# A retention and expert kernel on one core: shorter warm-up products, x by channels loaded from ScalarE's queue, two transfers at other points of SyncE's order

## What is computed

```python
x = x + attn(layernorm(x))     # q, k, v = x @ W.T; scores q.k times gamma_h ** (i - j) for j <= i, over sqrt(16)
                               # y = scores @ v; normalised over (time, channels of a head), scaled, shifted; @ W_o.T
x = x + ffn(layernorm(x))      # ((silu(x@sw1+sb1) * (x@sw3+sb3)) @ sw2 + sb2
                               #   + mean over k = 0, 1 of expert[(11*token + 7919*k) % 8](x)) / 2
# expert e: gelu(x @ w1[e] + b1[e]) @ w2[e] + b2[e]
```

## Time and profile before

| | before |
|---|---|
| median of three runs | 431.55 us (431.1 to 432.46) |
| the profiled execution | 431.59 us |
| its span, first to last instruction | 429.8 us |
| PE busy | 419.1 us, 98% of the span |
| DVE, ACT, POOL busy | 78%, 51%, 20% |
| granted TensorE clock | 9 tenths or more in all 40 slices |

### The profile page before, as it was taken

The page is one execution under the profiler, slowest core; times in us unless marked ns, Lnnn a source line. Parts: engine busy times, 40 slices in busy tenths (PEclk is TensorE's granted clock), DMA queues, the critical chain, the costliest instruction groups (busy, mean ns, idle before and its releaser), DMA issues.

```text
span 429.8 us, 14531 instructions
## 1 busy us (share of the span) xinstructions
PE 419.1 (98%) x6232; PEld 380.5 (89%) x6232; DVE 335.3 (78%) x791; ACT 219.2 (51%) x420; POOL 87.9 (20%) x78
## 2 busy tenths in 40 slices
PE   7998999999999989999999999999999999999997
PEld 5987899999998989998989988899888998888996
DVE  7888689876987788987798887978879878856423
ACT  3566667555754568345257325483344834346530
POOL 3062634532344232650510000100001000000000
PEclk9999999999999999999999999999999999999999
DMA  8554444434351232315450015100142001120011
GB/s 262 192 150 139 126 151 116 114 104 133 123 169 51 87 115 89 101 53 195 158 187 2 2 49 190 56 0 1 49 152 91 0 1 49 49 98 0 2 50 49
DMA packets 19769, 39.79 MB, mean 93 GB/s; under 512 B 3040, under 2 KB 5376, under 8 KB 19200
## 3 DMA queue, kind: packets, MB, share of 16 engines
q1 hardware_dynamic: 19280, 38.31, 27.5%
q10 hardware_dynamic: 432, 0.66, 0.5%
HBM read 30.55 MB, written 8.41 MB: 91 GB/s over the span
## 4 chain that ended last, share of the span: by engine, by line
PE 96%; issue 1%; DVE 1%; DMA 1%; POOL 0%; ACT 0%; DVEq 0%
PE bank L434 54%; PE bank L443 13%; PE bank L526 7%; PE bank L444 7%; PE bank L556 4%; PE bank L571 4%; PE bank L540 3%; PE bank L505 2%; PE bank L589 1%; DMA xin<-xa 1%; PE bank L647 0%; PE bank L461 0%; PE bank L452 0%; DVE xlo L1311 0%; DVE ln_st L1298 0%
## 5 line engine op out<-in xcount | busy, mean ns | idle before, releaser
L434 PE MATMUL bank<-x2lo,sw_hi 128*128 128x512 f32 x128 | 50.5, 394 | 0.0
L434 PE MATMUL bank<-x2hi,sw_lo 128*128 128x512 f32 x128 | 50.2, 392 | 0.0
L434 PE MATMUL bank<-x2hi,sw_hi 128*128 128x512 f32 x128 | 50.1, 392 | 0.0
L443 PE MATMUL bank<-w_both,ehi 128*128 128x512 f32 x124 | 45.1, 397 | 0.0
L887 ACT ACTIVATE sil<-bank,s1b 128x512 f32<-128x512 f32 x32 | 22.0, 687 | 45.0 <-PE bank L434 44.9
L443 PE MATMUL bank<-sw_both,ghi 128*128 128x512 f32 x124 | 44.9, 396 | 0.0
L1199 DVE STREAM_TRANSPOSE x2t<-xl 32x256 f32<-32x256 f32 x96 | 41.8, 436 | 1.8
L768 ACT ACTIVATE kexp<-bank 64x256 f32<-64x256 f32 x64 | 24.2, 378 | 30.9 <-PE bank L505 30.2
L1029 DVE TENSOR_TENSOR pm<-bank,msk 128x512 f32<-128x512 f32 x64 | 39.5, 679 | 0.0
L434 PE MATMUL bank<-xhi,wqkv_hi 128*128 128x256 f32 x128 | 38.0, 297 | 0.1
L906 ACT ACTIVATE ehi<-xres 128x512 fp32r<-128x512 f32 x32 | 20.3, 633 | 33.1 <-PE bank L444 32.6
(11 more groups left out here) (154 smaller groups left out, 1152.0 us busy)
## 6 DMA issues: line engine op xcount, KB each, us to landing
w_raw<-w SPq DMA_DIRECT2D x16, 256.0 KB, 3.3
xres<-xs SPq DMA_DIRECT2D x16, 256.0 KB, 3.4
x_scratch<-xres SPq DMA_DIRECT2D x16, 256.0 KB, 3.3
xl<-x_scratch SPq DMA_DIRECT2D x8, 512.0 KB, 4.5
xr<-x_scratch SPq DMA_DIRECT2D x4, 1024.0 KB, 4.8
xin<-xa SPq DMA_DIRECT2D x15, 256.0 KB, 3.0
out<-xr SPq DMA_DIRECT2D x7, 512.0 KB, 2.6
xin_t<-xt SPq DMA_DIRECT2D x13, 256.0 KB, 2.6
```

The costliest lines, as they stand in the source:

```text
L434: mm = nc.tensor.matmul(o, w[c][l], x[c][r], start=first and c == 0 and j == 0, stop=last and c == n - 1 and j == 2)
L443: nc.tensor.matmul(o.rearrange("p (k d) -> p k d", k=2), hi, w[c], start=c == 0, stop=c == n - 1, skip_group_check=True)
```

## The change

Four edits:

1. `WARM_UP` is 12 instead of 4, and each warm-up product has `CH` = 64 columns instead of 256.
2. `load_rstd(h + 2)` waits for `k_done` (k of part h + 1 projected) where it stood right behind the transfers of `sc_done`.
3. `load_xt` leaves SyncE, together with the wait for `kt_done`. ScalarE issues it in its step between `spread_k(h + 1)` and `copy_k(h + 1)`, with the same wait for `xlo_ready` from part 5 on.
4. In steps 8, 9, 12 and 13 the first of the two `next_xres` moves up from behind `y_done` to behind `q_done` and a new wait for `s_done` (the state sums of part h).

```diff
-WARM_UP = 4
+WARM_UP = 12
@@ block.sync
-            def load_xt(h):
-                if h >= TURNED + 2:
-                    sp.wait_ge(xlo_ready, h)
-                sp.dma_start(xin_t[h % 2][:], xt[h]).then_inc(xt_landed[h % 2], 16)
-
@@ block.sync, step(h)
                 if TURNED <= h + 2 < PARTS:
+                    sp.wait_ge(k_done, h + 2)
                     load_rstd(h + 2)
                 if h + 1 < PARTS:
                     sp.wait_ge(q_done, h + 2)
...
                     load_ffn(2 + LOAD_STEPS.index(h), 1)
-                if h + 1 < PARTS:
-                    sp.wait_ge(kt_done, h + 2)
-                if h + 3 < PARTS:
-                    load_xt(h + 3)
+                if b >= 2 and s < 2:
+                    sp.wait_ge(s_done, h + 1)
+                    next_xres(b - 1, 2 * s)
                 if h + 1 < PARTS:
                     sp.wait_ge(v_done, h + 2)
...
                 if b >= 2 and s < 2:
-                    next_xres(b - 1, 2 * s)
                     next_xres(b - 1, 2 * s + 1)
@@ block.tensor, warm_up(n)
-                    nc.tensor.matmul(c_bank[:, 0:2 * P], zeros[:, 0:P], zeros[:, 0:2 * P], start=True, stop=True)
+                    nc.tensor.matmul(c_bank[:, 0:CH], zeros[:, 0:P], zeros[:, 0:CH], start=True, stop=True)
@@ block.scalar
+            def load_xt(h):
+                if h >= TURNED + 2:
+                    act.wait_ge(xlo_ready, h)
+                act.dma_start(xin_t[h % 2][:], xt[h]).then_inc(xt_landed[h % 2], 16)
+
@@ block.scalar, step(h), behind spread_k(h + 1)
+                if h + 3 < PARTS:
+                    load_xt(h + 3)
                 if h + 1 < PARTS:
                     copy_k(h + 1)
```

## The result

The changed kernel takes 437.18 us (median of 6 runs, 434.63 to 439.19), the kernel before 431.16 in the same comparison. The ratio is 1.0143, 95% interval 1.0117 to 1.0170: **slower by 1.4%, 6 us**. I had forecast 430.8, so the sign was wrong and the time lies outside my range. The profiled execution has a span of 436.0 us (437.75 in all), against 429.8.

The account below looks back on a forecast made before the run. TensorE, busy 419.1 of 429.8 us, bounds the kernel, with 5.13 us lost to late instruction blocks. 431.59 - 0.9 (stops) + 0.15 (warm-up) = 430.8 us; own range 429.2 to 432.3, with rivals 427.6 to 433.6.

Parts of the forecast that it names:

- what the stops are: TensorE's "issue" gaps in the retention stage: late blocks of 256 instructions, 127 products apart; 5.13 us in all.
- The worst place I named: New short stretch of 2.15 us at 95.57, DMA share 0.62: a stop of 1.2 us near 97.7.
- My eight terms: Stops forecast for stretches at 19.73, 33.64, 36.60, 52.68, 70.59, 95.57, 127.97, 153.74; with 0.2 for two more, 4.2 us.
- x by channels on ScalarE: Issue of load_xt between spread_k and copy_k, in 13 steps: cost nothing, as ScalarE idles there for kt_done.
- the sum's main term: Late instruction blocks on TensorE, crossings 16 products earlier: stops 4.2 us against 5.13, so -0.9 us.
- warm-up as work: Start on TensorE: 24 records end near 6.3 where transposes began at 6.16, +0.15 us; bounds 0 and +1.1.
- rival B: Start: last warm-up product not far under 634 ns, transposes not started by 6.4; slower; chance 0.15.
- the shift: Warm-up count as instructions: every retention-stage crossing comes 16 products earlier, changing the stops by -0.9 us.
- My values lie between 0 and the bound: Each new stop valued between 0 and 5.2 us less its stretch, as a block needs 2.6 to 5.2 us.
- the moved transfers: load_rstd, next_xres and the waits: counted in the block needs, nothing of their own, between -0.5 and +0.5 us.

Follow-up runs that it names:

- e3: Changed kernel with the old warm-up (4 products of 256 columns) and 32 empty instructions behind it: 435.93 us, ratio 1.0132.
- e4: Kernel before with 32 empty instructions behind the warm-up, nothing else: 435.01 us, ratio 1.0106.
- e7: Kernel before with 16 empty instructions in front of TensorE's first wait, ahead of the warm-up: 434.36 us, ratio 1.0094.
- e8: Kernel before with load_xt moved to ScalarE's queue, without SyncE's wait for kt_done: 434.56 us, ratio 1.0091.
- the ladder: Ratios to before, adding edits: two moved transfers 0.9934; crossings 16 products earlier 1.0028; warm-up of 64 columns 1.0080; x early on ScalarE (changed kernel) 1.0143.
- the last pair of kernels: Changed kernel with load_xt held back on ScalarE by kt_done: warm-up of 64 columns 433.66 us (1.0080), of 128 columns 431.04 us (1.0028).
- e6: Kernel before with 12 warm-up products of 128 columns, no transfer moved: 433.42 us, ratio 1.0051.
- e10: Kernel before with load_xt on ScalarE's queue but behind the wait for kt_done, at its old time: 430.88 us, ratio 1.0003.
- e12: Kernel before with 4 warm-up products of 64 columns: 431.27 us, ratio 0.9992.

## Why the prediction was wrong, point by point

**Right: what the stops are.** The count of 127 products in a block, and that added instructions move the crossings 16 products earlier, hold in the changed kernel and in e3, e4 and e7. The stop of 2.32 us shrank but didn't go: 1.20 here, where I kept 0.1. The worst place I named, behind the stretch of 2.15 us, opened with 0.43 where I said 1.2 (1.75 in e4). The sum, 4.65 us in the profile, is near my 4.2, and that is luck. My eight terms 0.5, 0.6, 0.1, 0.3, 0.3, 1.2, 0.5 and 0.5 came out as 1.02, 0.26, 1.20, 0.81, 0.26, 0.43 and twice no stop over 0.25; one of eight is within 0.1.

**Wrong, step "x by channels on ScalarE": cost nothing.** Two errors. I took the issue on ScalarE to go out after `spread_k` ends. It goes out as it begins, in e8 at 40.12. I had looked for the cover on ScalarE (there was enough: ScalarE's wait for line 499 is 29.6 us in sum, 30.2 before) and not for what shares the DMA engines with the fetch of a block, although the sum's main term was about that fetch. The term is +2.7 us, from +0.63% in the ladder. That the fetch is what it disturbs remains argued.

**Wrong, step "warm-up as work": +0.15 us.** I let the clock rise at 5.2 us as before, and gave the other outcome, rival B, 0.15. B is what happened: the last warm-up product still takes 421 ns and the transposes begin at 7.2, where I had computed 7.3. B's price was 2.4 us; the profile has 2.9 at the transposes of k, and the last pair of kernels 2.2 at the end. I had quoted the Trainium skill against it (TensorE: Matmul & The Clock Gate, "What's actually happening": time, not number, of products). The measurement decides: 24 records of 64 columns without a gap in 5.2 us left the clock low in three kernels, and as many of 128 columns raised it in three, though in one only at their end.

**Missing: what a stop does to the clock.** I costed a stop at its own length. The traces show half-clock stretches behind stops among small products, 1.4 to 1.5 us each. The 20 profiles hold nine such stretches behind the start, and each begins 0.2 to 2.6 us behind the end of a stop of 0.6 to 2.15 us. The stop of 2.32 us before had none behind it, so a stop alone isn't enough, and I don't know the condition. This is the term that no step of mine had; it enters each step of the ladder in part.

**Mis-sized: the shift.** I put the shift at -0.9 us by adding up stops in one profile. It costs about 1 us in e6 (+0.51%, less a start 1.2 us later), 2 to 3 in e7 (+0.94%, less 0.9) and some 3.5 in the ladder, each with an uncertainty of 1.3 to 1.7 us. The step that failed is "My values lie between 0 and the bound": I read one execution of before as if its stops were fixed. They vary. The stop at product 855 is 2.32 us in one profile of before, 1.5 in e8, 1.39 in e10 and 0.84 in e12, none of which changes what stands in front by much, and runs of before range over 5 us. A sum of differences of such numbers can't carry 0.9 us.

**Wrong, step "the moved transfers": nothing of their own, between -0.5 and +0.5.** They gain 0.66%, 2.8 us, the only part that pays.

## What to carry to other kernels

Where the bounding engine has a long unrolled program, look in its chain for "issue" gaps at multiples of one distance in instructions: here they were late blocks of instructions. What helped here was to move transfers away from ahead of a crossing, and what hurt was an early transfer in a second queue. To add instructions in front, even idle ones, is a change to be measured too. A warm-up must be measured by the last product's length, not by its time on the chart. And an edit that only moves a transfer is to be costed by what it lands beside, at the time the queue issues it, which may be as the work ahead of it begins.

## What the runs showed of the hardware that I had not expected

- Plain float32 products of 64 columns with full loads of 128 weight columns, 24 records without a gap in 5.2 us, left TensorE at the pace of 1.2 GHz in three profiles; with 24 of 128 columns it was at 2.4 GHz by their end, 4.6 to 5.5 us, in three others.
- Behind a stop of 1.02 us among small products the granted clock fell to 0.50 for a stretch in which 24 split products took 4.16 us instead of 3.06.
- ScalarE issued a transfer as the first of the two activations ahead of it in the program began (40.12 against 40.11), before the second started (40.74).
- In the 20 profiles 90 of 94 stops over 0.25 us in TensorE's chain end 1.2 to 1.6 us behind the end of a transfer of 16 KB in the instruction queue.
- 256 KB more in each of 15 steps on SyncE's queue cost nothing (0.9994), in 13 steps on ScalarE's 0.85%.
- 16 instructions that do nothing, ahead of the warm-up, cost 0.94% (0.53 to 1.34), 3 to 4 us: 0.9 us of it is a later start, and the stops at the moved crossings are 1.5 us longer in sum.
